# A two-layer transformer kernel: each layer's order of steps as one loop body, gelu results written in place, gate rows by broadcast transfers

## What is computed

```python
gate = sign(gate) * max(|gate|, 0.25)             # both gates, both layers
# layer 0, per sequence
h  = layernorm(x) * (1 + scale1) + shift1
n  = rmsnorm(h) * norm_w
a  = [linear_attention(features(n Wq Wqf), features(n Wk Wkf), n Wv),  # 16 heads of 16, causal
      sliding_window_attention(n Wq, n Wk, n Wv)] @ Wout               # window of 64, softmax
x  = x + gate1 * (h + a)
h  = layernorm(x) * (1 + scale2) + shift2
x  = x + gate2 * sigmoid(mix_r(h) W_r) * (square(relu(mix_k(h) W_k)) W_v)   # mix: with the row before
# layer 1, per sequence
h  = layernorm(x) * (1 + scale1) + shift1
a  = softmax(rope(h Wq) rope(h Wk)^T / 4, causal) (h Wv) @ w_proj + b_proj
x  = x + gate1 * a
h  = layernorm(x) * (1 + scale2) + shift2
u  = silu(h w1^T s1) * (h w2^T s2)                 # 1024 wide
x  = x + gate2 * (gelu(gelu(u h1^T s) h2^T s) w3^T s)
```

## Time and profile before

| what | value |
|---|---|
| median of 3 runs (lowest, highest) | 2358.4 us (2356.93, 2362.96) |
| the profiled execution | 2359.58 us, its span 2357.6 us |
| mean granted TensorE clock | 0.958 |
| PE busy | 2074.8 us (88%), 17361 products |
| DVE, ACT, POOL busy | 1215.9 (52%), 923.7 (39%), 511.6 us (22%) |
| chain that ended last | PE 69%, DVE 17%, ACT 7%, issue 3% |
| transfers | 60.51 MB, mean 26 GB/s |

### The profile page before, as it was taken

One profiled execution on the slowest core, in us unless ns is written; L12 is line 12 of the kernel. 1 busy time (PEld: TensorE's weight loads), 2 busy tenths in 40 slices (PEclk: granted clock), 3 DMA queues, 4 the chain that ended last, 5 costly groups with the idle time before them and its releaser, 6 DMA issues.

```text
span 2357.6 us, 42193 instructions
## 1 busy us (share of the span) xinstructions
PE 2074.8 (88%) x17361; PEld 1491.3 (63%) x17361; DVE 1215.9 (52%) x2209; ACT 923.7 (39%) x1315; POOL 511.6 (22%) x676
## 2 busy tenths in 40 slices
PE   6788989999989888756698999999999999999998
PEld 4555555555555554524376777777767777777887
DVE  3435463645353453643555656655656656565443
...
GB/s 154 108 77 86 19 19 59 25 40 50 1 19 2 10 1 10 107 99 0 1 6 1 15 5 1 14 6 14 6 2 14 6 1 15 6 1 6 6 5 10
DMA packets 44894, 60.51 MB, mean 26 GB/s; under 512 B 13088, under 2 KB 35872, under 8 KB 44064
## 3 DMA queue, kind: packets, MB, share of 16 engines
...
## 4 chain that ended last, share of the span: by engine, by line
PE 69%; DVE 17%; ACT 7%; issue 3%; POOL 2%; DMA 1%; DVEq 0%; ACTq 0%; POOLq 0%
PE ps L1952 23%; PE ps L1879 4%; PE ps L1891 4%; DVE c_nat L1620 3%; PE ps L1098 3%; PE ps L1848 3%; PE ps L1066 3%; PE ps L1907 3%; PE ps L1126 3%; PE ps L1989 3%; PE ps L1017 2%; ACT a_probs L907 2%; PE ps L1146 2%; PE ps L1055 2%; PE ps L1052 2%
## 5 line engine op out<-in xcount | busy, mean ns | idle before, releaser
L1802 ACT ACTIVATE b_work<-ps,c_s 128x256 f32<-128x256 f32 x256 | 107.3, 470 | 462.1 <-PE ps L1952 462.0
L542 POOL TENSOR_SCALAR_AFFINE_SELECT a_probs<-a_probs 128x512 f32<-128x512 f32 (+1 forms) x224 | 160.9, 732 | 538.0 <-ACT a_probs L907 368.6
L1952 PEld LDWEIGHTS ps<-b_acts,b_h1T 128*128 128x128 f32 x2048 | 249.9, 191 | 27.5 <-issue 23.4
L1952 PE MATMUL ps<-b_acts,b_h1T 128*128 128x256 f32 x2048 | 265.8, 286 | 1.6 <-POOL b_acts L1556 1.1
L1952 PE MATMUL ps<-b_acts,b_h2T 128*128 128x256 f32 x2048 | 258.5, 285 | 2.0 <-DVE b_acts L1697 2.0
L1952 PEld LDWEIGHTS ps<-b_acts,b_h2T 128*128 128x128 f32 x2048 | 248.6, 192 | 15.1 <-issue 10.9
L907 ACT ACTIVATE a_probs<-ps 128x2048 f32<-128x2048 f32 (+1 forms) x96 | 153.0, 1593 | 129.9 <-PE ps L1066 127.1
L1548 POOL TENSOR_SCALAR_AFFINE_SELECT b_work<-b_work 128x512 f32<-128x512 f32 x128 | 80.4, 640 | 553.1 <-ACT b_work L1750 553.1
L1750 ACT ACTIVATE b_work<-ps 128x2048 f32<-128x2048 f32 (+1 forms) x96 | 153.1, 1594 | 103.0 <-PE ps L1891 102.9
L1620 DVE TENSOR_REDUCE c_nat<-ps 128x4 f32<-128x2048 f32 (+3 forms) x128 | 188.0, 1490 | 3.3
L1696 DVE CAST b_acts<-b_work 128x512 fp32r<-128x512 f32 x128 | 54.5, 426 | 227.9 <-ACT b_work L1802 227.9
(11 more groups left out here) (212 smaller groups left out, 3547.4 us busy)
## 6 DMA issues: line engine op xcount, KB each, us to landing
a_raw_next<-in_L_ffn_h_w SPq DMA_DIRECT2D x16, 512.0 KB, 3.8
...
a_x<-in_L_attn_x SPq DMA_DIRECT2D x8, 512.0 KB, 4.4
...
c_x<-x_mid SPq DMA_DIRECT2D x8, 512.0 KB, 4.0
...
```

Of the source, the lines that this page charges most:

```text
L542: return nc.gpsimd.affine_select(out=z, in_=z, compare_op=ALU.is_ge, fill=0.0, base=0, pattern=[[0, blocks_n], [1, cols]], channel_multipl ...
L1802: ins = nc.scalar.activation(full[nth % 2][:, j * HALF:(j + 1) * HALF], here[:, j * HALF:(j + 1) * HALF], ACT.Gelu, scale=s12[:, 2 + (name ...
L1952: ins = nc.tensor.matmul(dst, view(w[:, m, k]), view(src[:, k, i]), start=(k == 0 and i == 0), stop=(k == nk - 1 and i == 1))
```

## The change

1. Both planners go, with their costs, and two strings take their place, one for each layer. A string is one turn of a loop. `name.i.j+lag` is the step of pass (turn - lag), so neighbouring passes are interleaved inside one turn. `repeated` writes the turns out: turn after turn, leaving out steps whose pass isn't there.
2. The plan is all of layer 0's list followed by all of layer 1's. Layer 0's small rooms `m0` and `m1` are given out strictly in turn.
3. Gate rows: `rows` transposes all gates of a layer at once, ScalarE copies them, SP writes them to DRAM. From there SP loads each gate of each pass with a broadcast transfer. Layer 0's first `hg` stays with PE. Layer 1's `ga` step keeps only POOL's addition, now also behind `hn_ready`; `gb` is gone.
4. Gelu writes to `exact`, an f32 view of the same memory as `acts`, at the place of the second half of its result. The `full` buffers and the waits for them are gone from `att` and `h1`/`h2`.
5. A few waits take the place of orders that the planner used to secure (`heads`, `turn`).

```diff
+        self.gate_rows = [nc.dram_tensor(f"gate_rows{i}", (n * ND * B, P), F32, kind="Internal").ap() for i, n in enumerate((NMOD, NMOD + 1))]
+    def gate_row(self, layer, v, b):
+        rows = self.gate_rows[layer].rearrange("(v k b) d -> v b k d", k=ND, b=B)[v, b]
+        return rows.unsqueeze(0).broadcast_to([P, ND, P])
...
-COST0 = {"hg": 0.45, "ga": 0.25, "gb": 0.25, "hT": 0.45, "qk": 1.75, "v": 1.75, "tq": 0.45, "tk": 0.45, "fold": 0.9, "wm": 1.6, "again": 0.45,
...
+WT_PER_PASS = 7
+BODY0 = """
+tq.0 tk.0 win.3.1+1 turn.0+1 fold.0 wm.0.0 lv.3.1+1 lv.3.2+1 turn.2+1 wt.0+2 wm.0.1 wv.3.0+1 wv.3.1+1 lin.0.0 lh.3+1 v.0 again.0 lin.0.1 wh.3+1 v.1
+win.0.0 turn.1+1 tq.1 lv.0.0 tk.1 lin.0.2 turn.3+1 fold.1 wm.1.0 out.0+1 wm.1.1 stats-1 out.1+1 mod again.1 lin.1.0 wv.0.0 lv.0.1 win.0.1 wt.1+2
+lv.0.2 win.1.0 tq.2 lh.0 lv.1.0 lin.1.1 tk.2 fold.2 wv.0.1 wm.2.0 wt.2+2 rows.0-35 lv.1.1 wt.3+2 xT.0+1 rows.1+1 hg-1 wm.2.1 flag+8 xg wh.0 xT.1+1
+lin.1.2 wv.1.0 win.1.1 again.2 tq.3 lin.2.0 lv.1.2 r.0+1 lin.2.1 tk.3 fold.3 wv.1.1 lin.2.2 norm-1 lh.1 lv.2.0 wm.3.0 r.1+1 kk.0+1 wt.4+2 win.2.0 wh.1
+kk.1+1 hT.0-1 wm.3.1 hT.1-1 wt.5+2 lv.2.1 rms-1 win.2.1 again.3 qk.0-1 qk.1-1 wt.6+2 lin.3.0 wv.2.0 wv.2.1 lv.2.2 lin.3.1 wh.2 qk.2-1 last.0+1 win.3.0
+lh.2 last.1+1 qk.3-1 lin.3.2 lv.3.0
+"""
...
+            elif name == "rms" and b + 1 < B:
+                sp.wait_ge(rows_placed, 16)
+                sp.wait_ge(h_ready, NT * (b + 1))
+                load_gate(hg[:, 0], 1, b + 1, hg_ready)
+                load_gate(hg[:, 1], 0, b + 1, hg_ready)
+            elif name == "out" and step[2] and b + 1 < B:
+                sp.wait_ge(x1_ready, 2 * (b + 1))
+                load_gate(ga[:], 2, b + 1, ga_ready)
+            elif name == "kk" and step[2] and b + 1 < B:
+                sp.wait_ge(rg_ready, 2 * (b + 1))
+                load_gate(gb[:], 5, b + 1, gb_ready)
...
+BODY1 = """
+h1.0.3.1+3 values.1.1+2 values.1.2+2 max.3.1+2 h2.0.0.0+3 h2.0.0.1+3 h2.0.1.0+3 att.2.0+2 h2.0.1.1+3 h2.0.2.0+3 max.3.2+2 h2.0.2.1+3 h2.0.3.0+3
+h2.0.3.1+3 att.2.1+2 heads.1+2 split.1+3 last.0.0+3 again.3+2 values.2.0+2 att.2.2+2 stats+1 values.2.1+2 att.3.0+2 last.0.1+3 values.2.2+2 att.3.1+2
+heads.2+2 up.1.0+3 up.1.1+3 values.3.0+2 att.3.2+2 values.3.1+2 norm+1 up.1.2+3 up.1.3+3 values.3.2+2 hT+1 up.1.4+3 heads.3+2 up.1.5+3 proj.0+1
+proj.1+1 up.1.6+3 tq.0+1 tk.0+1 proj.2+1 tq.1+1 tk.1+1 up.1.7+3 proj.3+1 tq.2+1 tk.2+1 h1.1.0.0+3 tq.3+1 tk.3+1 h1.1.0.1+3 h1.1.1.0+3 turn.0+2
+max.0.0+1 h1.1.1.1+3 h1.1.2.0+3 max.0.1+1 h1.1.2.1+3 turn.1+2 h1.1.3.0+3 max.0.2+1 h1.1.3.1+3 out.0+2 again.0+1 max.1.0+1 h2.1.0.0+3 h2.1.0.1+3
+out.1+2 att.0.0+1 h2.1.1.0+3 h2.1.1.1+3 max.1.1+1 h2.1.2.0+3 h2.1.2.1+3 h2.1.3.0+3 h2.1.3.1+3 xT+2 split.0+2 last.1.0+3 att.0.1+1 last.1.1+3
+values.0.0+1 max.1.2+1 up.0.0+2 ga+1 up.0.1+2 att.0.2+1 up.0.2+2 again.1+1 max.2.0+1 up.0.3+2 up.0.4+2 values.0.1+1 values.0.2+1 att.1.0+1 up.0.5+2
+up.0.6+2 att.1.1+1 heads.0+1 up.0.7+2 values.1.0+1 att.1.2+1 h1.0.0.0+2 max.2.1+1 h1.0.0.1+2 h1.0.1.0+2 h1.0.1.1+2 max.2.2+1 h1.0.2.0+2 h1.0.2.1+2
+h1.0.3.0+2 again.2+1 max.3.0+1
+"""
...
-    first, slots, _ = order_layer0()
-    cut = max(i for i, step in enumerate(first) if step[0] in ("lv", "lh", "wv", "wh", "wt", "flag")) + 1
-    return [(0, step) for step in first[:cut]] + order_layer1(first[cut:]), slots
+    plan = repeated(BODY0, 0) + repeated(BODY1, 1)
+    slots, turn = {}, 0
+    for layer, step in plan:
+        if layer == 0 and step[0] in ROOM_OF:
+            slots[step] = ROOM_OF[step[0]]
+        elif layer == 0 and step[0] not in NO_ROOM:
+            slots[step] = ("m0", "m1")[turn]
+            turn = 1 - turn
+    return plan, slots
...
+            if name == "split" and step[2] == 0:
+                if b == 0:
+                    sp.wait_ge(first["x_sent"], 32 * B)
+                    load_weights("h2", "w3")
+                if b + 1 < B:
+                    sp.wait_ge(x1_ready, 2 * (b + 1))
+                    load_attention_gates(b + 1)
...
-                done = 16 * (b - 1) + 8 * (g // 2)
-                if g % 2 == 0 and j == 1 and done > 0:
-                    act.wait_ge(h_split, done)
...
-                if name == "h1" and i == 0:
-
-                    act.wait_ge(pv_done, min(3 * QUADS * (b + 1) + 6 * (half + 1), 3 * QUADS * B))
-                if nth >= 2:
-                    act.wait_ge(h_split, nth - 1)
+                dst = (exact_a if name == "h2" else exact_b)[:, 2 * i:2 * i + 2]
                 for j in range(2):
-                    ins = nc.scalar.activation(full[nth % 2][:, j * HALF:(j + 1) * HALF], here[:, j * HALF:(j + 1) * HALF], ACT.Gelu,
+                    ins = nc.scalar.activation(dst[:, j], here[:, j * HALF:(j + 1) * HALF], ACT.Gelu,
```

More of the change, by code:

```diff
@@ L135, in hold_layer0 @@
[L135 to L211, removed]
@@ L214 @@
[L214 to L218, removed]
@@ L1167, in modulate_next, with turn_gates @@
             ins.then_inc(full_sem, 1)
+        def turn_gates(step):
+            here, full_sem = take(step)
+            i = step[2]
+            if i:
+                pe.wait_ge(next_mod_ready, 1)
+            src = kept.modT if i else modT
+            nc.tensor.transpose(here[0:(NMOD + i) * ND * B, 0:P], src[:].rearrange("p v b -> p (v b)"), ident).then_inc(full_sem, 1)
         def turn_low(step):
@@ L1362, in slot_of, with entries, instance, repeated @@
     return "misc"
-def both_orders():
-    first, slots, _ = order_layer0()
-    cut = max(i for i, step in enumerate(first) if step[0] in ("lv", "lh", "wv", "wh", "wt", "flag")) + 1
-    return [(0, step) for step in first[:cut]] + order_layer1(first[cut:]), slots
+def entries(body):
+    for entry in body.split():
+        at = max(entry.find("+"), entry.find("-"))
+        words = (entry[:at] if at > 0 else entry).split(".")
+        name, index = words[0], [int(word) for word in words[1:]]
+        yield name, index, int(entry[at:]) if at > 0 else 0
+def instance(layer, name, index, b):
+    if layer:
+        return (name, b, *index)
+    if name in ONCE0:
+        return (name, 0, *index) if b == 0 else None
+    if name in QUAD0:
+        return (name, QUADS * b + index[0], *index[1:])
+    if name == "wt":
+        nth = WT_PER_PASS * b + index[0]
+        return (name, nth // 2, nth % 2) if nth < 2 * len(CHUNKS) else None
+    return (name, b, *index)
+def repeated(body, layer):
+    rows = list(entries(body))
+    late = [lag for _, _, lag in rows]
+    out = []
+    for turn in range(min(late), B + max(late)):
+        for name, index, lag in rows:
+            if 0 <= turn - lag < B:
+                step = instance(layer, name, index, turn - lag)
+                if step:
+                    out.append((layer, step))
+    return out
+def both_orders():
+    plan = repeated(BODY0, 0) + repeated(BODY1, 1)
[7 more added lines that the diff above has]
+    return plan, slots
 def fills_of(plan, slots):
@@ L1379, in fills_of @@
             continue
-        if layer == 1 and (name in ("split", "stats", "norm") or name in ("values", "last") and step[3] or name in ("h1", "h2") and step[4]):
+        if layer == 1 and (name in ("split", "stats", "norm", "ga") or name in ("values", "last") and step[3] or name in ("h1", "h2") and step[4]):
             continue
@@ L1657, in run @@
                 free = arrive(step)
+                if b and step[2] == 0:
+                    dve.wait_ge(hfull_ready, b)
                 src = room["misc"].rearrange("p (t h v) -> p t h v", t=NT, v=R)
@@ L1937, in project_out @@
                 ins.then_inc(full_sem, 1)
-            def gate_rows(step):
-                here, full_sem = take(step)
-                for i, v in enumerate((2, 6) if step[0] == "ga" else (5,)):
-                    for k in range(ND):
-                        ins = nc.tensor.transpose(here[:, i * D + k * P:i * D + (k + 1) * P],
-                                                  modT[:, v * ND + k, step[1]:step[1] + 1].broadcast_to([P, P]), ident)
-                ins.then_inc(full_sem, 1)
             def product(dst, w, m, src, nk, first):
```

270 lines of the change are left out of this document (60 added, 210 removed).

## The result

The change takes the kernel from 2357.66 us (2354.82 to 2362.96, 4 runs) to 2181.45 us (2181.36 to 2182.62, 4 runs): a ratio of 0.9251, 95% interval [0.9234, 0.9268]. The forecast was 2241 with a range from 2200 to 2308. The direction was right; the gain is 176 us where I had worked out 118, and the time lies 19 us under the low end. The profiled execution has a span of 2179.6 us and a mean granted clock of 0.965.

The account below looks back on a forecast made before the run. TensorE was taken to bound both layers' loops, with 9 to 11 us of bubbles per pass, and latency the seam. Start -1, layer 0 -64, seam +25, layer 1 with drain -78: -118 us, forecast 2241, range 2200 to 2308.

Parts of the forecast that it names:

- the term for layer 0: Layer 0's eight passes: 797.8 us busy, less 19.3, plus 52 idle, gives 830.5 for 894.4 today: -64 us.
- Why 4: Layer 0's five regular passes: 4 us of PE idle each, since part of the waits from in-order queues would stay.
- I take 7.6 of the 27 us that granted clocks cost: Layer 0: of 27 us lost today to granted clocks of 0.90 to 0.98, 7.6 us would be regained.
- the walk of the pairs: Products between neighbouring fills of one-buffer room `wide` against its hold: layer 0 short by 1.1 us before, 0.4 in BODY0.
- The one that I named as staying, `r.0`: Layer 0: `r.0` stands 4.9 us behind `xT.1`, while ScalarE's xT plus the mix take about 5.5; this wait stays.
- Layer 1: Layer 1's six regular passes: 148.5 us each, in all 965.5 down to 891, -75 us; its drain another -3.
- The seam: Between the layers, all of layer 0 now before layer 1: +25 us, with 47.7 us to layer 1's first transpose.
- Tables: ScalarE in layer 1: 28 more table loads, cost 0 as products cover them; without that cover 36 us.
- the two rivals that had every load paid or both rooms held: Layer 1: each added load stops PE, +64, 2305 us, chance 0.08; all eight changes per pass stop it, 2426, 0.05.
- Layer 0 keeps its bubbles: Rival: only layer 1 gains from the new order; layer 0 gives -19 instead of -64: 2286 us, chance 0.16.
- it doesn't do what it says: Rival: bubbles merely move in both loops; gates -20, seam +25, nothing else: 2364 us, chance 0.06.
- Gates' transfers: Gate rows by SP: each 128 KB transfer bounded at 0 to 4 us, taken as 2; cost 0, uncovered up to 56.

Follow-up runs that it names:

- e3: Changed kernel with layer 0 put back to its old planner's order, without gate steps; layer 1 keeps its new order: 2298.39 us.
- e9: Changed kernel with one step of layer 0's body, `r.0`, moved 2.7 us of products earlier: 2200.63 us.
- e10: Changed kernel with `r.0` moved two steps earlier than in e9, right after `lin.1.2`: 2227.55 us.
- e1: Changed kernel (gate rows by transfer, gelu in place) with both old planners and the old seam, without gate steps: 2341.6 us.
- e7: Changed kernel with layer 1's `max.0.1` moved to one h step behind `max.0.0` instead of two: 2188.3 us.
- e5: Changed kernel with layer 0's last turn and layer 1's first steps interleaved at the seam: 2154.39 us.
- e4: Changed kernel with Tanh in place of Gelu, so that layer 1's loop has no table loads: 2181.05 us.
- e2: Changed kernel with layer 1 put back to its old windows; layer 0 keeps its new loop body: 2251.21 us.

## Why the prediction was wrong in size and right in kind

**The step that failed** is the term for layer 0: "797.8 - 19.3 + 52 = 830.5: -64", and in it both numbers behind "Why 4" and "I take 7.6 of the 27 us that granted clocks cost". Measured, the stretch is 790.3 = 758.8 busy + 31.5 idle, 40 us less, and the two halves missed by about 20 us each.

*Idle*, 31.5 for 52. The five regular passes idle 2.1 us each for 4; the second 3.0 for 5; the last with its tail 3.0 for 11; the first 14.9 for 16. I had reasoned that the walk of the pairs explained only 1.1 of the old 9.5 us, so that most of it came from in-order queues, and that part of this would stay. It came from the order too: e3's list has a copy of qT, a mix, a first maximum (L808) and a mask that PE reaches too early, and with BODY0 all of these go. Of e3's four lines above, one stays: the wait of `lin` behind the second maximum, 4.7 us for 5.2. That the walk of `wide` does not see a bubble is no sign that an order can't remove it. The one that I named as staying, `r.0`, doesn't wait in a regular pass: e9 moved it 2.7 us earlier and it then waited 0.8, so it has 1.9 us to spare where I had found it 0.6 short.

*Busy*, 758.8 for 778.5. The clock's cost by the windows was 27 us and is now 0.13 x 102.1 = 13 us, all in the first pass: 14 gained, not 7.6. The mix's products, which stand behind a bubble in the old order, are 9.1 us of the fall (37.0 to 27.9); as far as they ran at half clock they are in the clock's 14 already. The gates' transposes are 10 to 12, as forecast. Some 14 us more of the fall are not split up, and what they are stays open. What e10 shows is that clock and bubbles are not two terms. Bubbles of 1.0 and 2.6 us close together brought half clock in every regular pass, and 0.7 and 1.6 did in e3's timeline; in e9 a bubble of 1.5 did not. So the term had to be made together: whoever forecasts that bubbles go which have a half-clock stretch behind them has forecast that these stretches go too.

**Layer 1** came out near the forecast: 147.6 us a pass for 148.5. e1 shows that the old order without gate steps takes 157, so the order is worth 58 of the 80 us, and e7 that a `max` fill put one half step early costs the bubble that the walk gives. In part the agreement is luck: the share of the gates was underrated (21 us, with 7 of waits and the clock's gain, for a forecast of 1.3 a pass, 8 in all) and that of the order overrated.

**The seam** has the right sign and its parts: 42.6 us to layer 1's first transpose for 47.7, 21.9 on to the first maximum for 21.5, 97.9 for the fills of pass 0 for 96, at a clock of 0.63, and then 60.6 where I had 72. These last 11 us are most of what the seam's forecast missed, and why they fell away is not shown. e5 shows that this loss, and more, was to be had back.

**Tables**: cost 0, as taken; e4 ends the two rivals that had every load paid or both rooms held. **Layer 0 keeps its bubbles** fell by e2, and **it doesn't do what it says** by the time itself and by e1: without the orders nine tenths of the gain are missing. **Gates' transfers** took 2.9 to 4.5 us for the 2 that I took and for a bound of 4, with the same result, since nothing waited for them.

**The range** missed by layer 0 alone. Its low end had +10 at the seam, as measured, and -88 for layer 1 with the drain, more than the -83 measured. For layer 0 it had only -80, which leaves 36 us of idle beside the same 19.3 of busy time: 24 us short, 20 by the busy time and 4 by the idle. The whole clock term (27 for 7.6) would have carried that end to 2181; it was not in it, though no row spoke against it.
